# Both layers of a spiking feed-forward network as three products of rounded parts

## The chip, the cores and the metric

One core of a Trainium2 chip. The kernel is one launch; its time is the device time in microseconds. The kernel before has a median of 658.88 us over 3 runs (658.28 to 659.46).

## The reference, cut to what matters

The model is two layers of a perceiver on x (16 x 64 x 256) with a context (16 x 1601 x 256): cross attention, a Mamba block, a spiking feed-forward network; then windowed attention over heads, a second attention, and eight experts of which two are added per token. The change is in the spiking network:

```python
h = jnp.square(jax.nn.relu(jnp.einsum('bsd,fd->bsf', x, W_fc)))   # x is layernormed; f = 1024
y = jnp.einsum('bsf,df->bsd', h, W_proj)                           # d = 256
def step(mem, _):
    reset = spike_fn(mem - 1.0)
    mem_new = 0.9 * mem + y - reset * 1.0
    return mem_new, spike_fn(mem_new - 1.0)
# five steps from mem = 0; the mean of the spikes is added to x
```

A spike is a comparison with a threshold, so y is wanted at nearly float32 precision.

## The kernel before, in words

The 1024 tokens are 8 tiles of 128; a quarter is two tiles (256 tokens, QT). One function, ffn_and_heads, holds the spiking network, the norms on either side and the attention over heads, because the engines work on all of it side by side. Each engine has one program, written out by hand in order at the end of its block; the engines meet only through counters: pe_steps, ac_steps and ve_steps list the order in which TensorE, ScalarE and VectorE complete their steps, and a wait names a step of such a list. GpSimd counts in s_z (its memsets), s_sn and s_v2.

Per quarter q the network goes so:

- TensorE turns the normed tokens of the quarter (turn_normed2, L1475) into a bank; ScalarE moves them to k.xT (move_turned2, L1822).
- TensorE's first_layer(q) (L1496) makes four blocks p = 4q to 4q+3 of 2 x 128 hidden features by 256 tokens, two float32 matmuls of 256 columns for each 128 features, in the two halves of one bank in turn. Block p waits for the relu of block p - 2.
- ScalarE's squares(q) (L1827) takes a relu (L1833) of the bank and writes its square (L1837) into hT, of which there are two. Squares of p wait for those of p - 2.
- TensorE's second_layer(q) (L1512) waits for the last square of the quarter and runs 2 x 8 float32 matmuls of 256 columns. ScalarE moves y (move_y, L1839).
- VectorE runs the five spike steps on y (spike, L2066, in five parts: 14 instructions of 128x512, most with two inputs in SBUF), adds them to x, takes the statistics (deviations3, L2100) and normalises (normalise3, L2109), which feeds the attention over heads.

Before it, VectorE adds the output of the Mamba block (residual2, L2035; deviations2, L2046) and normalises with two tensor_scalars a quarter (normalise2, L2055, instruction L2062). Quarters 0 and 1 come first; the projections of quarters 2 and 3 (out_proj, L1466) are done in this block, quarter 2 ahead of everything and quarter 3 behind first_layer(0).

The attention's own work is woven in: TensorE projects keys (L1522), values (L1535) and queries (project, L1556); VectorE adds the biases (keys, queries, L2122 to L2131); GpSimd multiplies with the sines and cosines (turn_pairs, L1991, three instructions a tile at L1999 to L2001, waiting for the queries' bias and running up to LEAD = 3 tiles ahead); VectorE adds the two products (rotate, L2133); TensorE turns them (turn_rotated, L1568). From step(0) (L1780) a pipeline over tiles i does scores, softmax and weighted values; the last quarter's spikes are run between its first steps. TensorE's order around the change stands at L1749 to L1787:

```python
            out_proj(2); turn_normed2(0); turn_normed2(1); first_layer(0); turn_normed2(2); out_proj(3)
            turn_value_bias(); second_layer(0); project_keys(0); project_value_bias(); first_layer(1)
            turn_normed2(3); project_values(0); second_layer(1); first_layer(2); turn_normed3(0)
            project_keys(1); project(0); second_layer(2); project(1); first_layer(3); turn_rotated(0, 0)
            turn_normed3(1); second_layer(3); turn_rotated(0, 1); project(2); turn_rotated(1, 0)
```

(one call a line in the code). The weights w_fc and w_pr (1 MB each) are loaded by SP long before, during the Mamba block. The experts at the end of the kernel (product, L2588; w_lo on GpSimd at L2847, on VectorE at L2864; rest_of_hidden, L3023) already use three products of rounded parts: a = hi + lo, with hi the value rounded to float32r by ScalarE and lo the rest, and a * b taken as hi*hi + hi*lo + lo*hi.

Of the kernel before, what the change touches and what calls it, by code (L numbers as in the profile page):

```python
# [6 lines left out]
F32 = mybir.dt.float32  # L7
# [7 lines left out]
P = 128  # L15
# [17 lines left out]
FF = 1024  # L33
# [1290 lines left out]
LEAD = 3  # L1324


def ffn_and_heads(nc, k):
# [7 lines left out]
    with ExitStack() as ctx:  # L1335
        sb, ps, sem = tools(nc, ctx)
        r_sb = [sb(f"r{i}", [P, 2, QT]) for i in range(2)]
        hT = [sb(f"fhT{i}", [P, FM, QT]) for i in range(2)]
# [18 lines left out]
        qT = [sb(f"q4T{i}", [P, HC, P]) for i in range(4)]  # L1357
        kT = [sb(f"k4T{i}", [P, HC, P]) for i in range(4)]
        mx = [sb(f"hmx{i}", [P, H]) for i in range(2)]
        sm = [sb(f"hsm{i}", [P, H, L]) for i in range(2)]  # L1360
        pT = sb("hpT", [P, H // 2, P])
# [49 lines left out]
        normed = (T[0], X, O, T[1])  # L1411
        n_pairs = float(L * L)
# [9 lines left out]
        sq = lambda q: [(w, 4 * q + n) for n in range(4) for w in ("re", "sq")]  # L1422
# [5 lines left out]
        ac_steps = [("r2", 1), ("x2", 0), ("x2", 1), ("r2", 2), *sq(0), ("x2", 2), ("cv", 0), ("r2", 3), ("y", 0),  # L1428
# [3 lines left out]
        ve_steps = [("rs", 1), ("st2", 1), ("ag2", 1), ("ep2", 1), ("rc2", 0), ("xn2", 0), ("rc2", 1), ("xn2", 1), ("rs", 2), ("st2", 2), ("ag2", 2),  # L1432
                    ("ep2", 2), ("rc2", 2), ("xn2", 2), ("rs", 3), ("st2", 3), ("ag2", 3), ("ep2", 3), ("rc2", 3), ("xn2", 3),
                    ("k", 0), ("cvec", 0), ("st3", 0), *nm(0), ("st3", 1), *nm(1), ("st3", 2), *nm(2), ("k", 1), ("k", 2),
# [22 lines left out]
        def _(e):  # L1457
# [25 lines left out]
            def turn_value_bias():  # L1483
                ac("x2", 1)
# [1881 lines left out]
```

## Time and profile before

| | before |
|---|---|
| median of 3 runs | 658.88 us |
| the profiled execution | 657.73 us |
| its span | 656.0 us |
| TensorE busy | 602.4 us (92%) |
| VectorE busy | 465.2 us (71%) |
| ScalarE busy | 368.7 us (56%) |
| GpSimd busy | 235.1 us (36%) |

The profile is one execution, and its span is what the engines' records cover; 1.73 us lie around it, and the execution is 1.15 us under the median of the runs. A float32 matmul of the program appears as two records of TensorE, a rounded one (float32r) as one; the type in a matmul's row reads f32 for both. PE is TensorE, PEld its weight loads, DVE VectorE, ACT ScalarE, POOL GpSimd. The name before the arrow is what is written: fhT is hT, hS the banks of both layers, r the relu, xz and mem the spikes' states. The block of ffn_and_heads begins at 369.9 us, its network ends at 444.8, the attention over heads at about 523.

### The profile page before, as it was taken

How to read it: one execution, taken by the hardware profiler on the slowest of the kernel's cores; microseconds unless marked ns; L12 is line 12 of the kernel's file. 1: busy time of each engine (PE TensorE's matmuls, PEld its weight loads, DVE VectorE, ACT ScalarE, POOL GpSimd, SP SyncE). 2: the span in 40 equal slices, each digit the busy share in tenths (PEclk: the TensorE clock that was granted, in tenths of full speed). 3: DMA queues.
4: the chain of work that ended last, by engine and by line, in shares of the span. 5: the costliest groups of instructions: out<-in, count | busy, mean ns of one | idle time of the engine just before them, and what ended most of it. 6: DMA issues, size and time to landing. Idle time of an engine off the chain costs nothing. (4 is left out here: it accounts for less than half of the span.)

```text
span 656.0 us, 11718 instructions
## 1 busy us (share of the span) xinstructions
PE 602.4 (92%) x4436; PEld 460.0 (70%) x4436; DVE 465.2 (71%) x798; ACT 368.7 (56%) x700; POOL 235.1 (36%) x190
## 2 busy tenths in 40 slices
PE   7999999999998778878788999999999899999997
PEld 6645555464366667767677888887777768889897
DVE  2753433347767999999999517788978878886554
ACT  2311111136889999999999333344656465555343
POOL 2000000000089999999898200035651022231000
PEclk8999999999999999999999999999999999999999
DMA  9999999984903232233220000000100022210001
GB/s 335 407 415 416 416 418 414 420 324 159 258 12 107 106 104 97 97 98 126 99 97 1 1 1 17 1 0 19 36 2 2 1 65 85 61 49 1 32 1 33
DMA packets 32831, 87.52 MB, mean 133 GB/s; under 512 B 8092, under 2 KB 20840, under 8 KB 30600
## 3 DMA queue, kind: packets, MB, share of 16 engines
q1 hardware_dynamic: 32088, 86.18, 35.7%
q8 instruction: 36, 0.59, 0.4%
q10 hardware_dynamic: 688, 0.59, 0.3%
q14 instruction: 19, 0.16, 0.1%
HBM read 84.53 MB, written 1.11 MB: 131 GB/s over the span
## 5 line engine op out<-in xcount | busy, mean ns | idle before, releaser
L847 POOL TENSOR_TENSOR dbu<-du,bs 128x1024 f32<-128x1024 f32 x64 | 149.8, 2365 | 7.0 <-DVE w_in L1095 4.6
L976 ACT ACTIVATE weighed<-T,CT 128x256 f32<-128x256 f32 x222 | 94.9, 592 | 1.2 <-PE T L1174 0.9
L1095 DVE TENSOR_TENSOR_SCAN w_in<-hS,dbu 128x1024 f32<-128x1024 f32 x42 | 94.6, 2271 | 0.4 <-ACT hS L965 0.4
L965 ACT ACTIVATE hS<-delta,negA 128x504 f32<-128x504 f32 x128 | 90.7, 813 | 5.3 <-DVE xn L1095 2.5
L1188 PE MATMUL Y<-ident,weighed 128*128 128x128 f32 x512 | 66.8, 273 | 0.1
L1174 PE MATMUL T<-ident,w_in 128*128 128x128 f32 x336 | 45.9, 279 | 19.8 <-ACT weighed L976 13.8
L1188 PEld LDWEIGHTS Y<-ident,weighed 128*128 128x128 f32 x512 | 57.8, 141 | 0.9 <-DVE sres L1119 0.3
L1174 PEld LDWEIGHTS T<-ident,w_in 128*128 128x128 f32 x336 | 36.1, 140 | 30.7 <-DVE w_in L1095 27.4
L1095 DVE TENSOR_TENSOR_SCAN xn<-hS,dbu 128x1024 f32<-128x1024 f32 x22 | 50.0, 2274 | 2.3 <-ACT hS L965 2.3
L425 POOL COPY w_xp<-w_xp 128x64 f32<-128x64 f32 x3 | 0.6, 234 | 138.8 <-DMA w_out<-in_w_out 138.8
L314 PE MATMUL O<-cN,pT 123*64 123x256 f32 (+1 forms) x384 | 46.7, 385 | 3.8 <-DMA cN<-in_ctx 3.1
L452 ACT ACTIVATE prob<-S,nbias 128x1601 f32<-128x1601 f32 x8 | 12.8, 1597 | 58.9 <-DVE nbias L601 58.9
L300 PE MATMUL S<-cT,qkT 128*64 128x512 f32 (+1 forms) x256 | 44.8, 502 | 0.9 <-DMA cT<-in_ctxT 0.7
L2784 ACT ACTIVATE hid<-BK,cols 128x512 f32<-128x512 f32 x32 | 22.0, 689 | 38.1 <-PE BK L2616 37.0
L3028 DVE TENSOR_TENSOR h_lo<-hid,h_hi 128x512 fp32r<-128x512 f32 x32 | 22.1, 693 | 28.6 <-ACT h_hi L2784 28.6
L314 PEld LDWEIGHTS O<-cN,pT 123*64 123x64 f32 (+1 forms) x384 | 25.4, 136 | 18.9 <-DMA cN<-in_ctx 5.0
L300 PEld LDWEIGHTS S<-cT,qkT 128*64 128x64 f32 x256 | 16.3, 136 | 30.1 <-issue 28.1
L2590 PE MATMUL BK<-w_hi,h_hi 128*128 128x256 f32 x128 | 37.1, 290 | 0.1
L594 DVE TENSOR_REDUCE mx<-S 128x1 f32<-128x1601 f32 x8 | 14.6, 1824 | 31.6 <-PE S L300 31.6
L2847 POOL TENSOR_TENSOR w_lo<-raw_w,w_hi 128x512 fp32r<-128x512 f32 x14 | 18.0, 1299 | 52.9 <-ACT w_hi L2727 52.9
L2590 PE MATMUL BK<-w_lo,h_hi 128*128 128x256 f32 x128 | 36.2, 283 | 0.0
L2590 PE MATMUL BK<-w_hi,h_lo 128*128 128x256 f32 x128 | 36.2, 283 | 0.0
(444 smaller groups left out, 1340.7 us busy)
## 6 DMA issues: line engine op xcount, KB each, us to landing
cN<-in_ctx SPq DMA_DIRECT2D x8, 3072.0 KB, 24.3
cT<-in_ctxT SPq DMA_DIRECT2D x7, 3202.0 KB, 24.5
bs<-b_rows SPq DMA_DIRECT2D x32, 512.0 KB, 3.7
raw_w<-in_w SPq DMA_DIRECT2D x16, 256.0 KB, 3.0
cT<-in_ctxT SPq DMA_DIRECT2D x1, 2178.0 KB, 12.2
cR<-in_ctx SPq DMA_DIRECT2D x8, 256.0 KB, 23.7
w<-in_w SPq DMA_DIRECT2D x7, 256.0 KB, 7.9
vs<-vx SPq DMA_DIRECT2D x8, 136.0 KB, 2.4
```

Of the source, the lines that this page charges most:

```text
L300: j = e.matmul(S[64 * b:64 * b + 64, c * HALF:c * HALF + w], qkT[:, kt, q:q + 64], cT[r][:, b, kt, c * HALF:c * HALF + w], start=kt == 0, ...
L314: j = e.matmul(O[64 * b:64 * b + 64, 0:D], pT[0:n_keys(c), c, 64 * b:64 * b + 64], v, start=c == 0, stop=c == ROWS)
L847: e.tensor_tensor(dbu[s % NB][:, :, :], half(m.du, s // DS), row, ALU.mult).then_inc(s_bu, 1)
L965: i = e.activation(by_batch(A[s % 2][:, j * HALF:(j + 1) * HALF]), by_batch(m.delta[:, c, h * HALF:(h + 1) * HALF]), ACT.Exp, scale=m.negA ...
L976: i = e.activation(weighed[s % 2][:, q * Q:(q + 1) * Q], T[:, q * Q:(q + 1) * Q], ACT.Copy, scale=c_of(s, q))
L1095: e.tensor_tensor_scan(S[s % NS], A[s % 2][:, :], dbu[s % NB][:, :, :].rearrange("p c n -> p (c n)"), 0.0, ALU.mult, ALU.add).then_inc(s_h, 1)
L1174: i = e.transpose(T[:, q * Q + j * P:q * Q + (j + 1) * P], S[s % NS][:, j * HALF + q * P:j * HALF + (q + 1) * P], k.ident[:, :])
L1188: i = e.matmul(Y[:, j * HALF + q * P:j * HALF + (q + 1) * P], weighed[s % 2][:, q * Q + j * P:q * Q + (j + 1) * P], k.ident[:, :], start=u ...
L2590: ins = e.matmul(dst, a, b, start=first and i == 0, stop=last and i == 2)
L2784: i = e.activation(dst, HB[m][:, :], ACT.Relu, bias=col(k, "b1", 2 * x + m))
L2847: e.tensor_tensor(k.w_lo[j // 2][:, j % 2, :, :], k.raw[j % SLOTS_W][:, :, :], k.w_hi[j // 2][:, j % 2, :, :].bitcast(F32), ALU.subtract). ...
L3028: e.tensor_tensor(h_lo[n % 2][:, m, :], hid[m][:, :], h_hi[n % 2][:, m, :].bitcast(F32), ALU.subtract).then_inc(s_l, 1)
```

## The change

Both layers are made of three products of rounded parts. Weights: ScalarE copies w_fc and w_pr rounded (fc_hi, pr_hi), GpSimd subtracts (fc_lo, pr_lo, four parts each). Tokens: ScalarE moves the turned tokens rounded (xT_hi), VectorE subtracts from the bank (low_part). Hidden features: ScalarE takes the relu, writes its square rounded (h_hi) and then unrounded over the relu; VectorE (10 blocks) or GpSimd (6 blocks: 4, 5, 8, 9, 12, 13) subtracts (low_square). There is one h_hi and one h_lo for all quarters, so squares of a quarter wait for the second layer of the quarter before. The second layer starts on the first rounded squares instead of the last, and asks for the rest block by block. The new tiles lie where later tiles of the attention lie, or over existing ones; the order of steps in the three lists changes with it.

```diff
+LO_AT = {p: 14 + i for i, p in enumerate((4, 5, 8, 9, 12, 13))}
...
+            fc_hi = part("fc_hi", [P, KD, FF], F32R)
+            x2_lo = [part(f"x2_lo{i}", [P, KD, QT], F32R) for i in range(2)]
+            pr_hi = part("pr_hi", [P, FM, D], F32R)
...
-        hT = [sb(f"fhT{i}", [P, FM, QT]) for i in range(2)]
+        h_hi, h_lo = (sb(n, [P, FM, QT], F32R) for n in ("fh_hi", "fh_lo"))
...
+        def lo_done(e, p):
+            if ("lo", p) in ve_at:
+                e.wait_ge(s_fv, ve_at["lo", p])
+            else:
+                e.wait_ge(s_z, LO_AT[p])
...
             def first_layer(q):
                 tok = slice(q * QT, (q + 1) * QT)
                 ac("x2", q)
+                ac("whi", 0)
...
-                        m = 2 * n + u
+                        cols = slice((2 * n + u) * P, (2 * n + u + 1) * P)
+                        dst = fp[p % 2][:, u * QT:(u + 1) * QT]
                         for c in range(KD):
-                            j = e.matmul(fp[p % 2][:, u * QT:(u + 1) * QT], k.w_fc[:, c, m * P:(m + 1) * P],
-                                         k.xT[:, c, tok], start=c == 0, stop=c == 1)
+                            e.matmul(dst, fc_hi[:, c, cols], k.xT_hi[:, c, tok], start=c == 0, stop=False)
+                            if q == 0 and u == 0 and c == 0:
+                                e.wait_ge(s_z, 4 + p)
+                            e.matmul(dst, k.fc_lo[:, c, cols], k.xT_hi[:, c, tok], start=False, stop=False)
+                        if n == 0 and u == 0:
+                            ve("xl", q)
+                        for c in range(KD):
+                            j = e.matmul(dst, fc_hi[:, c, cols], x2_lo[q % 2][:, c, :], start=False, stop=c == 1)
                     done(j, "fc", p)
...
             def second_layer(q):
-                ac("sq", 4 * q + 3)
                 if q >= 2:
                     ac("y", q - 2)
                 for u in range(2):
+                    dst, tok = yp[q % 2][:, u * D:(u + 1) * D], slice(u * P, (u + 1) * P)
                     for m in range(FM):
-                        j = e.matmul(yp[q % 2][:, u * D:(u + 1) * D], hT[q % 2][:, m, u * P:(u + 1) * P], k.w_pr[:, m, :],
-                                     start=m == 0, stop=m == FM - 1)
+                        if u == 0 and m % 2 == 0:
+                            ac("hi", 4 * q + m // 2)
+                            if q == 0:
+                                e.wait_ge(s_z, 8 + m // 2)
+                        e.matmul(dst, h_hi[:, m, tok], pr_hi[:, m, :], start=m == 0, stop=False)
+                        e.matmul(dst, h_hi[:, m, tok], k.pr_lo[:, m, :], start=False, stop=False)
+                    for m in range(FM):
+                        if u == 0 and m % 2 == 0:
+                            lo_done(e, 4 * q + m // 2)
+                        j = e.matmul(dst, h_lo[:, m, tok], pr_hi[:, m, :], start=False, stop=m == FM - 1)
...
             def squares(q):
...
                     if p >= 2:
-                        e.wait_ge(s_fa, ac_at["sq", p - 2])
-                    done(e.activation(r_sb[p % 2][:, :, :], fp[p % 2].rearrange("p (u n) -> p u n", u=2), ACT.Relu), "re", p)
-                    if q >= 2:
-                        pe("pr", q - 2)
+                        lo_done(e, p - 2)
+                    r = r_sb[p % 2][:, :, :]
+                    done(e.activation(r, fp[p % 2].rearrange("p (u n) -> p u n", u=2), ACT.Relu), "re", p)
+                    if q:
+                        pe("pr", q - 1)
                     e.wait_ge(s_fa, ac_at["re", p])
-                    done(e.activation(hT[q % 2][:, 2 * n:2 * n + 2, :], r_sb[p % 2][:, :, :], ACT.Square), "sq", p)
+                    done(e.activation(h_hi[:, 2 * n:2 * n + 2, :], r, ACT.Square), "hi", p)
+                    e.wait_ge(s_fa, ac_at["hi", p])
+                    done(e.activation(r, r, ACT.Square), "sq", p)
...
+            e.wait_ge(k.s_w3, k.n_w3)
+            done(e.activation(fc_hi[:, :, :], k.w_fc[:, :, :], ACT.Copy), "whi", 0)
             root2(1)
+            done(e.activation(pr_hi[:, :, :], k.w_pr[:, :, :], ACT.Copy), "whi", 1)
             move_turned2(0)
...
+            e.wait_ge(s_fa, ac_at["whi", 0])
+            for n in range(FM // 2):
+                cols = slice(2 * n * P, (2 * n + 2) * P)
+                e.tensor_tensor(k.fc_lo[:, :, cols], k.w_fc[:, :, cols], fc_hi[:, :, cols].bitcast(F32),
+                                ALU.subtract).then_inc(s_z, 1)
+            e.wait_ge(s_fa, ac_at["whi", 1])
+            for n in range(FM // 2):
+                ms = slice(2 * n, 2 * n + 2)
+                e.tensor_tensor(k.pr_lo[:, ms, :], k.w_pr[:, ms, :], pr_hi[:, ms, :].bitcast(F32), ALU.subtract).then_inc(s_z, 1)
             e.wait_ge(s_fp, pe_at["out", 3])
             for r in range(2):
                 e.memset(v2[r][:, :, :, :, :], 0.0).then_inc(s_z, 1)
...
-            for t in range(LEAD):
+            for q in (1, 2):
+                for n in range(2):
+                    low_square(4 * q + n)
+            turn_pairs(0)
+            for n in range(2):
+                low_square(12 + n)
+            for t in range(1, LEAD):
                 turn_pairs(t)
...
+            def low_part(q):
+                ac("x2", q)
+                if q >= 2:
+                    pe("fc", 4 * (q - 2) + 3)
...
+            def low_square(p):
+                q, n = divmod(p, FM // 2)
+                ms = slice(2 * n, 2 * n + 2)
+                ac("sq", p)
+                if q:
+                    pe("pr", q - 1)
+                done(e.tensor_tensor(h_lo[:, ms, :], r_sb[p % 2][:, :, :], h_hi[:, ms, :].bitcast(F32), ALU.subtract), "lo", p)
```

VectorE's order gets low_part(0) and (1) behind the residual of quarter 2, low_square(0) to (3) behind the normalising of quarter 2, low_part(2) behind that of quarter 3, low_part(3) behind normalise3(0), and low_square(6), (7), (10), (11), (14), (15) between the last parts of the spikes of quarters 0, 1 and 2: 6, 10 and 14 ahead of 7, 11 and 15, with one part of the spikes between the two of a pair. The waits of TensorE on a token move ("x2") that guard a bank become waits on the subtraction ("xl") that now reads it last.

## Rows read from the trace of the kernel before

**Rows 1.** Page, part 1: the engines' busy time, share and instructions.

```profile
PE 602.4 (92%) x4436; PEld 460.0 (70%) x4436; DVE 465.2 (71%) x798; ACT 368.7 (56%) x700; POOL 235.1 (36%) x190
```

**Rows 2.** Stretches, all engines: length, busy us (instructions) of PE, PEld, DVE, ACT, POOL, clock, DMA.

```profile
375.00:446.00 71.00, 70.46 (x338) 61.63 (x338) 44.34 (x94) 27.19 (x50) 7.62 (x8) 1.00 0.02 5
...
474.00:520.00 46.00, 44.32 (x673) 35.33 (x674) 35.53 (x81) 27.02 (x44) 12.04 (x27) 1.00 0.01 2
```

**Rows 3.** Timeline of TensorE, first layer of quarter 1: start, us, engine, line, operation.

```profile
395.55 7.07 PE L1508 MATMUL hS<-xT,w_fc 128*128 128x256 f32 x32
402.45 0.60 PE L1479 MATMUL hT<-ident,xn 128*128 128x128 f32 x4
```

**Rows 4.** Timeline of TensorE, an expert's second layer: its first row, the row behind it.

```profile
590.07 0.28 PE L2590 MATMUL BK<-w_hi,h_hi 128*128 128x256 f32 x1
...
592.95 1.03 PE L2570 MATMUL BK<-ident,xn 128*128 128x128 f32 x8
```

**Rows 5.** Timeline of ScalarE, a block's relu and square, and the next relu.

```profile
397.47 0.60 ACT L1833 ACTIVATE r<-hS 128x512 f32<-128x512 f32 x1 [3.72 <-PE hS L1508]
398.11 0.63 ACT L1837 ACTIVATE fhT<-r 128x512 f32<-128x512 f32 x1
```

**Rows 6.** ScalarE, one line's durations (ns, least/median/most), then a row of its timeline.

```profile
L2727 ACT ACTIVATE w_hi<-raw_w x16: 612/626/654, 533.1 to 595.5; 128x512 fp32r<-128x512 f32 x16
...
455.92 1.06 ACT L1885 ACTIVATE hsm<-hsm 128x1024 f32<-128x1024 f32 x1
```

**Rows 7.** Two lines' durations in the experts, ns least/median/most: subtractions of VectorE, of GpSimd.

```profile
L3028 DVE TENSOR_TENSOR h_lo<-hid,h_hi x32: 681/693/716, 544.4 to 647.8; 128x512 fp32r<-128x512 f32 x32
...
L2847 POOL TENSOR_TENSOR w_lo<-raw_w,w_hi x14: 1263/1284/1456, 534.8 to 596.2; 128x512 fp32r<-128x512 f32 x14
```

**Rows 8.** Timeline of GpSimd, then of VectorE beside it, at 555 us.

```profile
554.79 4.02 POOL L2847 TENSOR_TENSOR w_lo<-raw_w,w_hi 128x512 fp32r<-128x512 f32 x3 [7.89 <-ACT w_hi L2727]
...
556.28 1.40 DVE L2909 SCALAR_TENSOR_TENSOR ady<-cn,ady 128x256 f32<-128x256 f32 x1
...
559.13 0.42 DVE L2914 TENSOR_TENSOR ok<-ok,causal 128x256 f32<-128x256 f32 x1
```

**Rows 9.** Timeline of GpSimd, then of VectorE beside it, at 434 us.

```profile
433.29 1.68 POOL L1999 TENSOR_TENSOR w_in<-qkb,trig 128x512 f32<-128x512 f32 x1 [5.75 <-DVE qkb L2130]
...
433.73 1.79 DVE L2089 SCALAR_TENSOR_TENSOR xz<-mem,xz 128x512 f32<-128x512 f32 x1
...
436.68 1.10 DVE L2083 SCALAR_TENSOR_TENSOR xz<-mem,y 128x512 f32<-128x512 f32 x1
```

**Rows 10.** Timelines at the start: VectorE, TensorE, ScalarE.

```profile
372.03 0.73 DVE L2062 TENSOR_SCALAR xn<-x,mv,rstd 128x256 f32<-128x256 f32 x2
...
374.08 0.60 PE L1479 MATMUL hX<-ident,xn 128*128 128x128 f32 x4
374.93 7.17 PE L1508 MATMUL hS<-xT,w_fc 128*128 128x256 f32 x32 [0.25 <-ACT xT L1824]
...
374.28 0.60 ACT L1824 ACTIVATE xT<-hT 128x512 f32<-128x512 f32 x1 [2.12 <-PE hT L1479]
```

**Rows 11.** Timeline of VectorE from y of quarter 1 to that of quarter 2's spikes.

```profile
412.36 0.69 DVE L2083 SCALAR_TENSOR_TENSOR xz<-y 128x512 f32<-128x512 f32 x1 [5.57 <-ACT y L1843]
...
427.58 0.76 DVE L2139 TENSOR_TENSOR hrot<-w_in 128x256 f32<-128x256 f32 x2 [2.81 <-POOL w_in L2001]
429.20 0.69 DVE L2083 SCALAR_TENSOR_TENSOR xz<-y 128x512 f32<-128x512 f32 x1 [0.86 <-ACT y L1843]
...
438.31 0.68 DVE L2090 SCALAR_TENSOR_TENSOR mem<-mem,xz 128x512 f32<-128x512 f32 x1
```

**Rows 12.** Kernel's start: stretches (columns as in rows 2).

```profile
8.00:10.00 2.00, 1.81 (x14) 1.82 (x15) 1.63 (x8) 0.77 (x2) 0.00 (x0) 0.85 1.07 420
10.00:12.00 2.00, 2.00 (x7) 1.64 (x6) 1.17 (x4) 0.48 (x2) 0.00 (x0) 0.50 1.01 405
12.00:14.00 2.00, 1.97 (x10) 1.44 (x9) 0.07 (x1) 0.65 (x2) 0.00 (x0) 0.79 1.01 394
```

More of the change, by code:

```diff
@@ L1336, in ffn_and_heads @@
         sb, ps, sem = tools(nc, ctx)
+        with ExitStack() as before_heads:
+            part = tools(nc, before_heads)[0]
+            fc_hi = part("fc_hi", [P, KD, FF], F32R)
+            x2_lo = [part(f"x2_lo{i}", [P, KD, QT], F32R) for i in range(2)]
+            pr_hi = part("pr_hi", [P, FM, D], F32R)
+        late = sb("qk4T", [P, 4, HC, P])
+        sm = [sb(f"hsm{i}", [P, H, L]) for i in range(2)]
+        pT = sb("hpT", [P, H // 2, P])
         r_sb = [sb(f"r{i}", [P, 2, QT]) for i in range(2)]
-        hT = [sb(f"fhT{i}", [P, FM, QT]) for i in range(2)]
+        h_hi, h_lo = (sb(n, [P, FM, QT], F32R) for n in ("fh_hi", "fh_lo"))
         y = [sb(f"y{i}", [P, 2 * D]) for i in range(2)]
@@ L1356, in ffn_and_heads @@
         rot = [sb(f"hrot{i}", [P, 2 * H, SPAN]) for i in range(2)]
-        qT = [sb(f"q4T{i}", [P, HC, P]) for i in range(4)]
-        kT = [sb(f"k4T{i}", [P, HC, P]) for i in range(4)]
+        qT = [sb(f"q4T{i}", [P, HC, P]) for i in range(2)] + [late[:, i, :, :] for i in range(2)]
+        kT = [sb(f"k4T{i}", [P, HC, P]) for i in range(2)] + [late[:, 2 + i, :, :] for i in range(2)]
         mx = [sb(f"hmx{i}", [P, H]) for i in range(2)]
-        sm = [sb(f"hsm{i}", [P, H, L]) for i in range(2)]
-        pT = sb("hpT", [P, H // 2, P])
         warm = sb("hwarm", [P, 1])
@@ L1421, in ffn_and_heads @@
         fc = lambda q: [("fc", 4 * q + n) for n in range(4)]
-        sq = lambda q: [(w, 4 * q + n) for n in range(4) for w in ("re", "sq")]
+        sq = lambda q: [(w, 4 * q + n) for n in range(4) for w in ("re", "hi", "sq")]
         nm = lambda q: [("ag3", q), ("ep3", q), ("rc3", q), ("xn3", q), ("cx", q)]
@@ L1526, in project_keys @@
                 else:
-                    ac("x2", 2)
+                    ve("xl", 2)
                 for u in range(2):
@@ L1535, in project_values @@
             def project_values(p):
-                ac(*(("x2", 0), ("x3", 1), ("x3", 2), ("v", 2))[p])
+                if p == 0:
+                    ve("xl", 0)
+                else:
+                    ac(*(("x3", 1), ("x3", 2), ("v", 2))[p - 1])
                 for u in range(2):
@@ L1823, in move_turned2 @@
                 pe("t2", q)
-                done(e.activation(k.xT[:, :, 2 * q * P:(2 * q + 2) * P].rearrange("p c (u n) -> p c u n", u=2),
+                done(e.activation(k.xT_hi[:, :, 2 * q * P:(2 * q + 2) * P].rearrange("p c (u n) -> p c u n", u=2),
                                   normed[q][:, :].rearrange("p (u c n) -> p c u n", u=2, c=KD), ACT.Copy), "x2", q)
@@ L2040, in residual2 @@
                 done(e.tensor_tensor(x, x, fp[1] if g == 1 else normed[g][:, :], ALU.add), "rs", g)
+                if g == 2:
+                    low_part(0)
+                    low_part(1)
                 own("rs", g)
@@ L2280, in _ @@
                 normalise2(q)
+                if q == 2:
+                    for n in range(FM // 2):
+                        low_square(n)
+            low_part(2)
             spike(0, 0)
@@ L2287, in _ @@
             spike(0, 3)
+            low_square(6)
             spike(0, 4)
+            low_square(7)
             deviations3(0)
             normalise3(0)
+            low_part(3)
             spike(1, 0)
@@ L2293, in _ @@
             spike(1, 2)
+            low_square(10)
             spike(1, 3)
+            low_square(11)
             spike(1, 4)
@@ L2303, in _ @@
             spike(2, 2)
+            low_square(14)
             spike(2, 3)
+            low_square(15)
             spike(2, 4)
@@ L3111, in perceiver @@
         k.xn = sb("xn", [P, TILES, D])
+        with ExitStack() as rounded:
+            k.xT_hi = tools(nc, rounded)[0]("xT_hi", [P, KD, TOK], F32R)
         k.xT = sb("xT", [P, KD, TOK])
@@ L3258, in perceiver @@
         k.c0T = sb3("c0T", [P, KD, TOK])
+        with ExitStack() as rounded:
+            k.fc_lo = tools(nc, rounded)[0]("fc_lo", [P, KD, FF], F32R)
         k.w_fc = sb3("w_fc", [P, KD, FF])
+        with ExitStack() as rounded:
+            k.pr_lo = tools(nc, rounded)[0]("pr_lo", [P, FM, D], F32R)
         k.w_pr = sb3("w_pr", [P, FM, D])
```

26 lines of the change are left out of this document (19 added, 7 removed).

## The prediction

> **What bounds the kernel now.** I read the page's shares first: TensorE is busy 92% of the span [rows 1]. Then the stretches: in 375 to 446 us, which holds both layers of the spiking network, TensorE works 70.46 of 71.00 us, VectorE 44.34, ScalarE 27.19, GpSimd 7.62 at full clock; in the attention steps behind it (474 to 520 us) TensorE still works 44.32 of 46.00 [rows 2]. So a microsecond taken from or added to TensorE's path there reaches the end: the blocks behind start when this one ends, and I found nothing with slack between. Last the timelines, for what stands beside TensorE: VectorE waits for y of each quarter, then runs its own chain (spikes, normalising, rotation), and waits again. That slack is what the change spends.
>
> **TensorE's own term.** A group of one layer and quarter is 16 float32 matmuls of 256 columns, seen as 32 records; groups follow each other after 6.90 us [rows 3], 0.431 each. The change makes them 48 rounded ones of the same shape. The experts' second layer has exactly these: 24 between 590.07 and 592.95, 0.120 each [rows 4]. So 5.76 us a group, 1.14 less; eight groups give -9.1 us if nothing else binds. The Trainium skill (TensorE: Matmul & The Clock Gate, Back-to-back issue gap) gives N/2.4 + 2.5 ns, 109 ns at 256 columns; the row says 120, and by 109 the sum below would end near 1 us lower. The row decides.
>
> **ScalarE.** Relu takes 0.60, its square 0.63, each waiting for the one before [rows 5]: 1.23 a block. With the second square a block takes 0.64 + 0.66 + 0.54 (the next relu starts while the last square ends) = 1.84, against TensorE's new 1.44. New too are two copies of 128x2048. From 0.626 for 512 columns rounded [rows 6] and 1.06 for 1024 [rows 6], 0.9 ns a column: 2.0 us each. ScalarE is idle then, so the first runs 369.9 to 371.9, the second to 374.1, just ahead of the first move of turned tokens at 374.28 [rows 10]: cost nothing, and without that cover 2 us each.
>
> **GpSimd and VectorE get in each other's way, and this decides.** GpSimd gets 8 subtractions of weights and 6 of squares, 1.28 us each; VectorE 10 of squares at 0.69 (0.60 apart) [rows 7], and 4 of the transposed tokens at the same. While GpSimd ran three of its subtractions back to back (554.79 to 558.81, 1.34 each), a 256-column instruction of VectorE took 1.40 instead of the 0.42 of the one behind them [rows 8]: one GpSimd instruction is let by for one of VectorE's, in turn. The same in this stage: with GpSimd's three products at 433.29, three 0.68 us instructions of VectorE, the first 1.79 and the third 1.10 long, took from 433.73 to 437.78 [rows 9], 4.05 us instead of 1.9 at 0.60 apart: a loss of 2.1. So each 1.28 us subtraction on GpSimd costs VectorE 1.0 to 1.2 where VectorE reads two tensors of SBUF or runs a tensor_scalar, nothing where it reads PSUM. The Trainium skill (SBUF — State Buffer) tells it as an exclusive lock held for a whole instruction, which speaks against this change; the rows agree, so it changes no number.
>
> **The walk.** I follow TensorE's order and carry the shift against before.
> 1. Start. GpSimd's first subtraction begins at 371.94 behind the first copy, VectorE's normalising at 372.03 [rows 10]. Its four tensor_scalars each wait for one GpSimd instruction: 1.0 + 1.2 + 1.0 + 1.2 = 4.3, less 0.4 that they stood ready before the transposes. The second transposes come at 377.9 instead of 374.08 and stand ahead of the first layer, which starts at 378.35 instead of 374.93: **+3.4**. Bounds: 0 if VectorE always goes first, 4.3.
> 2. Quarter 0. Residual 2 and its statistics are behind these and two token subtractions, so the root and with it the first relu come 1 us after the matmuls, and ScalarE's 1.84 a block then leads: the first layer gains nothing (+3.4). Second layer: -1.1, **+2.2**.
> 3. Quarter 1. First layer -1.1. Two GpSimd subtractions (blocks 4, 5) hold the spikes up by 2, and blocks 6 and 7 stand in VectorE's order; block 7 is ready at 409.8, TensorE wants it at 408.2: 1.6 of waiting against 1.1 of gain. **+1.6**.
> 4. Quarter 2. First layer -1.1 (+0.4); then the query projection waits for the tokens' move, queued on ScalarE behind 4 x 1.84: +1.8. Second layer -1.1: **+1.1**. First layer of quarter 3: -1.1, +0.5 for the queries of tile 0: **+0.4**.
> 5. Second layer of quarter 3. It needs VectorE's blocks 14 and 15, after the spikes of quarter 2. VectorE from y of quarter 1 to that place took 412.36 to 438.91 = 26.6 us, with 0.86 of waiting for y that goes [rows 11] (the 2.81 behind GpSimd's products stays). It adds four subtractions of its own (2.4), 2.0 for GpSimd's blocks 8 and 9, 2.1 for 12 and 13, 0.3 around. From 413.8 that gives 446.3, where TensorE waits since 440.1. 26 matmuls remain, 3.1: done issuing at 449.4 instead of 444.7: **+4.8**.
> 6. The rotation of tile 2 and the keys come late behind the spikes of quarter 3: +0.9, after that the steps keep the shift: **+5.8**.
> 7. Clock. TensorE has two thin stretches, 373.5 to 378.35 and 440.1 to 446.3. At the kernel's start, behind waits for the first loads, the granted clock fell to 0.85, 0.50 and 0.79 of full in three stretches of 2 us [rows 12], 2 x (0.15 + 0.50 + 0.21) = 1.7 us lost between its levels of 2.4 and 1.2 GHz. Bounds 0 and 2 x 1.7 here; I take one fall, at the second and longer stretch, part of it spent in the wait: **+1.2**.
>
> Costs of nothing: the weight parts are there before they are used (first at 373.2 wanted at 378.5, last of the second layer at 382.8 wanted at 390.7); TensorE's new waits on copies and token parts fall behind later ones; the memsets of v2 keep their place after the projection; GpSimd's rotation of tile 0 stands behind blocks 8 and 9, done at 419.8, before its queries, and tile 1 behind 12 and 13 is part of step 5. No DMA is added or moved; SP waits on the moved values as before.
>
> **Sum.** +5.8 + 1.2 = +7.0: span 656.0 to 663.0, the profiled execution 657.73 to 664.7; it stood 1.15 under the median of 658.88, so 665.9.
>
> **Rivals.**
> A, VectorE first: if the first copy ends after 372.03, or VectorE's instruction wins the tie, one or two of the four waits at the start go. For it: 0.09 us decides. +3.7 to +4.9 before the clock: 662.6 to 663.8.
> B, VectorE keeps up in quarter 3: GpSimd and VectorE overlap more than rows 9 show, so step 1 or step 5 loses its waiting. Walked with one of the two free, the shift is +1.5 to +2.5: 660.4 to 661.4. Against it: both rows show whole turns.
> C, faster: the turns hardly cost, the rounded matmuls pay. The turns are some 11 us of new waiting on VectorE (4.3 at the start, 1.1 behind it, 2.0, 2.1, the rest smaller); the sign changes once more than about 6 of them are gone, and with none at all the walk ends 6.2 to 8.4 under: 650.5 to 652.7. For it: all 32 of VectorE's subtractions in the experts took 0.68 to 0.72 [rows 7]. Against: GpSimd did nothing beside them, and where it did [rows 8, 9] the turns are whole.
> D, the clock falls twice, or long after the second stretch: +8.5 to +10: 667.4 to 669. The Trainium skill (TensorE: Matmul & The Clock Gate, HAM oscillation) has idle gaps in TensorE's work fall back to half clock, each time again; here that is D in full.
> E, the rounded products are not at 0.120: at 0.125 it is +0.5, at 0.108 -1.2; inside the forecast.
>
> **Chances.** Forecast 0.56, A 0.12, B 0.12, D 0.10, C 0.10. The range runs from B's lower middle to D: 660.8 to 669.0; it leaves out C, half of B's edge and D's tail. A measurement here can tell 0.2%, 1.3 us, from no change. Faster by more: C, 0.10. Within: B's lowest, 0.04. Slower: the rest, 0.86.
>
> **What would show it.** Step 1: normalising at L2062's place with durations of 1.3 to 1.6 us, and the first layer at 378. Step 3: TensorE waiting about 1.6 us for a subtraction of VectorE. Step 5: a wait of about 4 us and one of about 1.7 in the last second layer, released by VectorE, spikes at 1.1 to 1.8 us. Step 7: granted clock under 1.00 behind it. TensorE's groups at 5.76 where nothing waits. I am wrong if the waits at L2062's place stay at 0.41, if the last second layer runs through, or if a group takes more than 6.9 us unbroken.

## The result, and the profile after

| | before | after |
|---|---|---|
| median | 659.14 us (658.28 to 659.46, 4 runs) | 664.94 us (664.60 to 665.55, 4 runs) |
| the profiled execution | 657.73 us | 664.60 us |
| its span | 656.0 us | 662.6 us |

The ratio of after to before is 1.0094, 95% interval 1.0082 to 1.0107: 0.9% slower, 1 us under the forecast of 665.9 and inside its range. The profiled executions differ by 6.87: 6.6 of span and 0.27 around it. Before's profiled execution was quicker than its median, so medians differ by 5.8 only.

The page of the changed kernel, its shares and the granted clock in 40 slices (compare [rows 1]):

```profile
PE 599.8 (91%) x4564; PEld 462.9 (70%) x4564; DVE 484.2 (73%) x812; ACT 381.4 (58%) x718; POOL 254.6 (38%) x204
...
PEclk9999999999999999999999899988999999999999
```

The stretch of both layers (columns as in [rows 2]):

```profile
375.00:446.00 71.00, 60.29 (x439) 57.49 (x440) 57.70 (x100) 35.40 (x64) 23.26 (x20) 0.94 0.02 5
```

TensorE has lost what bound it: 60.29 busy of 71 us where it had 70.46, while VectorE went from 44.34 to 57.70. Where it went, in the timeline of the start; ScalarE, GpSimd, VectorE, TensorE, and ScalarE's first blocks:

```profile
369.44 1.91 ACT L1963 ACTIVATE fc_hi<-w_fc 128x2048 fp32r<-128x2048 f32 x1 [0.47 <-PEq L706]
...
371.43 5.09 POOL L2026 TENSOR_TENSOR fc_lo<-w_fc,fc_hi 128x512 fp32r<-128x512 f32 x4 [0.28 <-ACT fc_hi L1963]
...
371.53 2.60 DVE L2146 TENSOR_SCALAR xn<-x,mv,rstd 128x256 f32<-128x256 f32 x2
...
374.23 2.44 DVE L2146 TENSOR_SCALAR xn<-x,mv,rstd 128x256 f32<-128x256 f32 x2
...
374.18 0.66 PE L1495 MATMUL hT<-ident,xn 128*128 128x128 f32 x4 [0.88 <-DVE xn L2146]
376.72 1.11 PE L1495 MATMUL hX<-ident,xn 128*128 128x128 f32 x4 [1.89 <-DVE xn L2146]
377.49 0.56 PE L1526 MATMUL hS<-xT_hi,fc_hi 128*128 128x256 f32 x1
...
380.49 0.58 ACT L1869 ACTIVATE r<-hS 128x512 f32<-128x512 f32 x1
381.10 0.63 ACT L1873 ACTIVATE fh_hi<-r 128x512 fp32r<-128x512 f32 x1
381.76 0.63 ACT L1875 ACTIVATE r<-r 128x512 f32<-128x512 f32 x1
382.30 0.58 ACT L1869 ACTIVATE r<-hS 128x512 f32<-128x512 f32 x1
```

VectorE normalises with two pairs of instructions. A pair took 0.73 us before [rows 10]; now the two take 2.60 and 2.44 us beside GpSimd's row of subtractions. TensorE waits 0.88 and 1.89 us for them and starts the first layer at 377.49; it was 374.93 [rows 10], in a block that began 0.5 us later (VectorE's first instruction there is at 369.96 before, at 369.46 after).

Then quarters 1 to 3: two groups of the first layer with what stands behind each, TensorE's waits for low parts, and VectorE beside GpSimd:

```profile
396.68 0.47 PE L1526 MATMUL hS<-xT_hi,fc_hi 128*128 128x256 f32 x1
...
402.55 0.60 PE L1495 MATMUL hT<-ident,xn 128*128 128x128 f32 x4
...
409.01 0.51 PE L1551 MATMUL hS<-pr_hi,fh_lo 128*128 128x256 f32 x2 [1.51 <-DVE fh_lo L2114]
...
412.18 0.28 PE L1526 MATMUL hS<-xT_hi,fc_hi 128*128 128x256 f32 x1
...
417.86 0.60 PE L1587 MATMUL hT<-ident,xn 128*128 128x128 f32 x4
...
443.47 0.80 PE L1551 MATMUL hS<-pr_hi,fh_lo 128*128 128x256 f32 x2 [3.84 <-DVE fh_lo L2114]
445.40 0.79 PE L1551 MATMUL hS<-pr_hi,fh_lo 128*128 128x256 f32 x2 [1.13 <-DVE fh_lo L2114]
445.99 0.41 PE L1546 MATMUL hS<-pr_hi,fh_hi 128*128 128x256 f32 x1
...
433.48 1.46 POOL L2071 TENSOR_TENSOR fh_lo<-r,fh_hi 128x512 fp32r<-128x512 f32 x1 [2.02 <-ACT r L1875]
435.35 1.29 POOL L2071 TENSOR_TENSOR fh_lo<-r,fh_hi 128x512 fp32r<-128x512 f32 x1 [0.41 <-ACT r L1875]
438.33 1.68 POOL L2049 TENSOR_TENSOR w_in<-qkb,trig 128x512 f32<-128x512 f32 x1 [1.69 <-DVE qkb L2214]
...
433.82 1.67 DVE L2167 SCALAR_TENSOR_TENSOR xz<-mem,y 128x512 f32<-128x512 f32 x1
435.42 1.77 DVE L2173 SCALAR_TENSOR_TENSOR xz<-mem,xz 128x512 f32<-128x512 f32 x1
...
438.76 1.79 DVE L2173 SCALAR_TENSOR_TENSOR xz<-mem,xz 128x512 f32<-128x512 f32 x1
440.48 1.20 DVE L2174 SCALAR_TENSOR_TENSOR mem<-mem,xz 128x512 f32<-128x512 f32 x1
441.72 1.09 DVE L2167 SCALAR_TENSOR_TENSOR xz<-mem,y 128x512 f32<-128x512 f32 x1
442.73 0.68 DVE L2114 TENSOR_TENSOR fh_lo<-r,fh_hi 128x512 fp32r<-128x512 f32 x1
...
444.65 0.69 DVE L2114 TENSOR_TENSOR fh_lo<-r,fh_hi 128x512 fp32r<-128x512 f32 x1
```

The groups run in 5.87 and 5.68 us where 6.90 stood [rows 3]. Each GpSimd subtraction makes one spike instruction of VectorE 1.7 to 1.8 us instead of 0.69, and the three rotation products three more. Blocks 14 and 15 are subtracted at 442.73 and 444.65; TensorE, which has run out of other matmuls by 439.6, waits 3.84 and 1.13 us. Behind that its matmuls are 0.21 apart: half clock.

### The profile page after: what moved, and what is told of

Same layout as the page of the kernel before. It is cut to its first block and busy times, and to the rows that moved or that the text cites. A ratio compares the mean times of both kernels' runs of the same rounds, so it can differ in the third digit from the quotient of the medians.

```text
span 662.6 us, 12043 instructions
## 1 busy us (share of the span) xinstructions
PE 599.8 (91%) x4564; PEld 462.9 (70%) x4564; DVE 484.2 (73%) x812; ACT 381.4 (58%) x718; POOL 254.6 (38%) x204
## 3 DMA queue, kind: packets, MB, share of 16 engines
HBM read 84.53 MB, written 1.11 MB: 129 GB/s over the span
```

## The experiments

How far each kernel's events lie behind those of the kernel before, in us, from ScalarE's timeline of each profile: y of quarters 0 to 3, the first exponential of the heads (455.92 before), the second move of v (531.03), the turned phases' move (562.41), and the span (656.0). The column "start" has the first instruction of VectorE in the block of the network (369.96 before): nothing that was edited comes before it, it differs between profiles by itself, and every later column contains it. The names are those of the experiments below.

| profile | start | y0 | y1 | y2 | y3 | first exp | v | phases | span |
|---|---|---|---|---|---|---|---|---|---|
| after | -0.50 | +1.32 | +0.65 | +0.51 | +6.42 | +6.54 | +6.59 | +6.59 | +6.6 |
| start_later | -0.49 | -1.97 | -2.62 | -2.77 | +2.07 | +2.08 | +3.12 | +4.60 | +4.6 |
| weights_memset | -0.50 | -1.44 | -2.10 | -2.23 | +2.52 | +2.52 | +3.51 | +4.99 | +4.9 |
| all_memset | -0.32 | -1.74 | -3.64 | -4.06 | -2.59 | -2.57 | -1.59 | -0.10 | -0.1 |
| clock_fill | -0.26 | +1.53 | +0.89 | +2.30 | +3.97 | +4.79 | +4.81 | +6.29 | +6.2 |
| first_only | +0.13 | +3.43 | +2.21 | +0.99 | -0.24 | -0.24 | +0.81 | +0.81 | +0.8 |
| first_later | -0.14 | -0.82 | -2.04 | -3.26 | -4.49 | -4.48 | -3.43 | -3.40 | -3.4 |
| second_only | +0.09 | -1.13 | -1.80 | -1.92 | +3.52 | +3.53 | +4.57 | +4.60 | +4.6 |
| ve_all | +0.03 | -1.43 | -3.88 | -1.53 | -1.49 | -0.53 | +0.52 | +2.04 | +2.0 |
| before_again | -0.15 | -0.16 | -0.16 | -0.16 | -0.16 | -0.15 | -0.12 | +1.35 | +1.3 |
| after_again | -0.35 | +2.53 | +1.88 | +3.32 | +6.82 | +6.83 | +7.90 | +7.89 | +7.9 |
| first_later_fill | -0.14 | -0.81 | -2.04 | -3.27 | -4.51 | -4.50 | -4.50 | -4.50 | -4.5 |
| before_shift | +0.72 | +2.27 | +2.27 | +2.28 | +2.27 | +2.27 | +2.27 | +3.79 | +3.8 |

Read it in two halves. Up to the first exponential the columns tell what the edit does, mixed with the falls of the clock in that stretch. From there on all kernels run the same work (first_later_fill has its transposes at the end of the block besides), and the shift still grows by 1.0 at v or by 1.5 at the phases in some profiles and not in others; that is the clock, below.

### start_later: the weights' remainders wait for the normalising

```diff
             e.wait_ge(s_fa, ac_at["whi", 0])
+            e.wait_ge(s_fv, ve_at["xn2", 1])
             for n in range(FM // 2):
                 cols = slice(2 * n * P, (2 * n + 2) * P)
```

> The eight weight subtractions of GpSimd wait until VectorE has normalised quarters 0 and 1; nothing else is changed. Theory of the turns: in the changed kernel VectorE's four normalising instructions take 2.60, 2.60, 2.44 and 2.44 us beside these subtractions (0.7 before), and the first layer of quarter 0 begins at 377.49 instead of 374.93 less 0.5. Without them beside, VectorE's four are back at 0.41 each, the walk of the orders gives 3.8 us less than the changed kernel, and the stretch of a low granted clock at 376 to 380 has no wait ahead of it any more: 660.3 to 661.3. Rival, ScalarE is the bound (three activations for each block, 1.82 us): it starts no later and then sets the pace, so what is won at the start is lost by the end of quarter 1: 664 to 665. Rival, the granted clock alone: the gain is that of the first low stretch, below 1 us.

Measured: 662.97 us (before beside it 658.31), ratio 1.0072 [1.0054, 1.0091]. The timeline of VectorE and GpSimd at its start:

```profile
371.54 0.73 DVE L2147 TENSOR_SCALAR xn<-x,mv,rstd 128x256 f32<-128x256 f32 x2
...
372.38 0.73 DVE L2147 TENSOR_SCALAR xn<-x,mv,rstd 128x256 f32<-128x256 f32 x2
...
373.27 5.01 POOL L2027 TENSOR_TENSOR fc_lo<-w_fc,fc_hi 128x512 fp32r<-128x512 f32 x4 [2.10 <-DVE xn L2147]
```

Both pairs are back at 0.73. At the first exponential the kernel is 4.46 us ahead of the changed one, +2.08 against before, or +2.57 counted from the block's start; the walk gave +2.0. ScalarE as the bound of the whole is out: the lead at the start (3.29 us at y of quarter 0) is still 3.27 and 3.28 at those of quarters 1 and 2. The turns of the weights are not gone but moved: the pair that normalises quarter 2 now takes 2.21 us, the first low square 1.78. The time fell less than expected, by some 1.5 us (1.0094 to 1.0072; the two intervals overlap, so the medians alone hardly tell it), to 1.7 us above the top of what was expected, and the table says where: +1.04 and +1.48 came back in the experts, where nothing was edited.

### weights_memset and all_memset: the same places, no operand read

```diff
-                e.tensor_tensor(k.fc_lo[:, :, cols], k.w_fc[:, :, cols], fc_hi[:, :, cols].bitcast(F32),
-                                ALU.subtract).then_inc(s_z, 1)
+                e.memset(k.fc_lo[:, :, cols].bitcast(F32), 0.0).then_inc(s_z, 1)
```

and the same for pr_lo; in all_memset also for h_lo in GpSimd's low_square. These kernels leave the low parts out of the result.

> Leaves out the remainders of the weights: GpSimd writes zeros where it subtracted, eight times, with the same semaphores; TensorE's work is the same. Theory of the turns: an instruction that only writes does not hold VectorE up, so the four normalising instructions take about 0.41 us each and the time is that of the kernel whose subtractions start later, 660.3 to 661.3. If a write of zeros holds VectorE up like a subtraction, the time stays at 664 to 665.

> Leaves out the remainders of the weights and of six of the sixteen squares: GpSimd writes zeros in place of all fourteen subtractions, same semaphores, same work on TensorE and ScalarE. Theory of the turns: no spike instruction of VectorE is over 0.75 us between 395 and 445, blocks 14 and 15 come in time, and the walk gives 9 us less than the changed kernel: 655 to 657, below the kernel before. Rival, ScalarE's third activation is the bound: its block of 1.82 us is unchanged, so 660 to 662, the gain of the start alone.

Measured: weights_memset 662.70, ratio 1.0063 [1.0046, 1.0079]; all_memset 657.98, ratio 0.9986 [0.9971, 1.0001], 1.4 and 1.0 us above what was expected. Weights_memset, GpSimd and VectorE at the start:

```profile
371.41 2.21 POOL L2026 MEMSET fc_lo<- 128x512 f32 x4 [0.25 <-ACT fc_hi L1963]
...
371.53 1.62 DVE L2145 TENSOR_SCALAR xn<-x,mv,rstd 128x256 f32<-128x256 f32 x2
...
373.26 1.11 DVE L2145 TENSOR_SCALAR xn<-x,mv,rstd 128x256 f32<-128x256 f32 x2
```

and all_memset, GpSimd and VectorE in quarter 2:

```profile
430.71 0.53 POOL L2070 MEMSET fh_lo<- 128x512 f32 x1 [1.34 <-ACT r L1875]
431.20 1.47 POOL L2048 TENSOR_TENSOR w_in<-qkb,trig 128x512 f32<-128x512 f32 x1
...
430.82 0.68 DVE L2172 SCALAR_TENSOR_TENSOR xz<-mem,xz 128x512 f32<-128x512 f32 x1
431.42 1.80 DVE L2173 SCALAR_TENSOR_TENSOR mem<-mem,xz 128x512 f32<-128x512 f32 x1
...
434.28 1.21 DVE L2113 TENSOR_TENSOR fh_lo<-r,fh_hi 128x512 fp32r<-128x512 f32 x1
```

TensorE's waits for VectorE's low parts in all_memset, from 368 to 460 (total, times, longest):

```profile
PE hS L1551 <- DVE fh_lo L2113: 2.2, 3, 1.4
```

The expectation was half wrong: a memset of 0.54 us does hold up a tensor_scalar (the four lost 1.3 us in all; beside subtractions 3.6), but not a two-input spike instruction (0.68 beside the memset, 1.80 beside the product). From weights_memset to all_memset only the six squares change, and the first exponential comes 5.1 us sooner: those turns were the larger part. With both gone the kernel is 2.57 ahead of before at that place (2.25 from the block's start; walk 3.2), not the 9.1 of TensorE's own term. Part of the rest is in the profile: the rotation products still make spike instructions of 1.80 and 1.10 us and a low square of 1.21, against the 0.75 that was expected at most, TensorE still waits 2.2 us for VectorE's low parts, and the clock fell behind these waits (0.53 at 438 to 441). How much ScalarE's block of 1.82 us and VectorE's ten subtractions keep by themselves is not shown.

### first_only, first_later, second_only: one layer at a time

In first_only the second layer is the old one; first_later adds the wait of start_later; second_only has the old first layer.

```diff
-            h_hi, h_lo = (sb(n, [P, FM, QT], F32R) for n in ("fh_hi", "fh_lo"))
+            hT = [sb(f"fhT{i}", [P, FM, QT]) for i in range(2)]
...
-                        e.matmul(dst, h_hi[:, m, tok], pr_hi[:, m, :], start=m == 0, stop=False)
-                        e.matmul(dst, h_hi[:, m, tok], k.pr_lo[:, m, :], start=False, stop=False)
+                        j = e.matmul(yp[q % 2][:, u * D:(u + 1) * D], hT[q % 2][:, m, u * P:(u + 1) * P], k.w_pr[:, m, :],
+                                     start=m == 0, stop=m == FM - 1)
```

> The change for the first layer alone: rounded parts of its weight and its input as in the changed kernel; the second layer is the kernel before's float32 one (one square, two hT buffers, no low squares, no rounded w_pr), and the start is not delayed. Theory of the turns: the start loses 3.0 us to the four subtractions of w_fc beside VectorE's normalising, the first layers of quarters 1 to 3 win 1.14 us each, and VectorE has only four instructions more, so the second layer of quarter 3 waits for nobody: the walk gives 0.5 us less than the kernel before at the end of the stretch, 657 to 659.5 with one fall of the clock at the start. Rival, the square's three activations and the second layer's products were what paid: then first-layer products alone give no gain over the changed kernel, 663 to 666.

> As the kernel with the change for the first layer alone, and GpSimd's four weight subtractions wait until VectorE has normalised quarters 0 and 1. Theory of the turns: the start costs nothing and each of the four first layers wins about 1.1 us; the walk gives 4.3 us less than the kernel before at the end of the stretch: 653.5 to 655.5, and up to 2.5 more where the granted clock falls at 525 and 557 us, as it did in three kernels whose stretch ended at another time than those of the kernels before and changed: at most 658. Rival, first-layer products don't pay: 658 or more with no fall.

> The change for the second layer alone: rounded w_pr, three activations for a block, sixteen low squares on VectorE and GpSimd in the places that the changed kernel gives them; the first layer is the kernel before's float32 one with no rounded input or weight. Theory of the turns: the start is free, but VectorE and GpSimd hold each other up in quarters 1 to 3 as in the changed kernel and TensorE waits for the low parts of blocks 14 and 15: the walk gives 2.5 us more than the kernel before, and the fall of the clock at that wait 1 to 2.5 more: 661 to 663.5. Rival, the loss is the start's alone: at or below the kernel before, 655 to 659.

Measured beside a before of 659.13: first_only 658.66, ratio 0.9998 [0.9982, 1.0014]; first_later 654.87, ratio 0.9944 [0.9925, 0.9963]; second_only 663.14, ratio 1.0071 [1.0047, 1.0096]. At the first exponential -0.24, -4.48 and +3.53 stand beside the walk's -0.5, -4.3 and +2.5, the last without the fall of the clock that its expectation put at 1 to 2.5 more. The stretch of first_later, and TensorE's waits in second_only from 368 to 460 (total, times, longest):

```profile
375.00:438.00 63.00, 62.41 (x384) 57.33 (x384) 44.13 (x89) 25.60 (x47) 11.26 (x11) 1.00 0.02 5
```

```profile
PE hS L1542 <- DVE fh_lo L2089: 4.9, 3, 3.5
```

With the first layer alone TensorE hardly waits (62.41 busy of 63.00 us) and for no low part: all four groups' 1.14 arrive, 4.5 us, and VectorE has four instructions more instead of fourteen. With the second layer alone the wait of quarter 3 is there without any trouble at the start. So the change is two: a half that pays, once its start is delayed, and a half that costs, in this order of the engines' work.

### ve_all: all sixteen low squares on VectorE

The wait of start_later, no low_square on GpSimd, and VectorE's order so (q1, for example):

```diff
             spike(1, 0)
+            low_square(8)
             spike(1, 1)
             spike(1, 2)
-            low_square(10)
+            low_square(9)
             spike(1, 3)
-            low_square(11)
             spike(1, 4)
+            low_square(10)
             deviations3(1)
+            low_square(11)
             normalise3(1)
```

> Both layers as in the changed kernel; GpSimd's weight subtractions wait for the normalising of quarters 0 and 1, and all sixteen low squares are VectorE's, spread over its order a little after the blocks (GpSimd has none). VectorE has six instructions of 0.69 us more than in the changed kernel (4.1 us). Theory of the turns: each of GpSimd's 1.28 us subtractions cost VectorE 1.0 to 1.2 us, so giving them up costs VectorE nothing, and the order brings blocks 14 and 15 sooner: the walk gives 1.9 us less than the kernel before at the end of the stretch, 656 to 658, up to 2.5 more with falls of the clock later. Rival, VectorE's load is the bound, whoever holds it up: 4.1 us more than the kernel whose subtractions start later (663.0), 665 to 667.

Measured: 657.47 (655.57 to 660.14 in ten runs), ratio 0.9979 [0.9960, 0.9998]. Giving VectorE 4.1 us more work of its own made the kernel 5 to 6 us faster than start_later, where it should have slowed it if VectorE's load were the bound. The order was changed with it (the low squares, and the low part of quarter 3's tokens, which moved behind the queries' bias), so how much of this is the turns' alone is not separated here; all_memset is the run for that. TensorE waits for no low part any more; it waits 2.9 us for the move of normed tokens, which stands on ScalarE behind the triple activations. The walk's -1.9 was -0.53: in this profile the clock fell there too, at 417 to 423 and 444 to 450. Beside the same runs of before the first layer alone, started late, has the lower median (0.9944 against 0.9979, intervals that overlap by 0.0003), so no run here shows the second layer's products paying.

### clock_fill: work for TensorE in the wait

```diff
+                        if q == 3 and u == 0 and m in (4, 6):
+                            for _ in range((0, 0, 30, 8)[m // 2]):
+                                e.transpose(fp[0][:, 0:P], k.ident[:, :], k.ident[:, :])
                         if u == 0 and m % 2 == 0:
                             lo_done(e, 4 * q + m // 2)
```

> Adds 38 transposes of the identity into a free PSUM bank, ahead of TensorE's waits for the low parts of blocks 14 (30 of them) and 15 (8) in the second layer of quarter 3; nothing else is changed. Theory that the low clock after that wait (0.90 at 438 to 442, 0.50 at 442 to 449, 0.60 at 449 to 452) costs time of its own: the granted clock stays at 1.00 from 438 to 455, the matmuls behind the wait are back at 0.12 us each, and the time falls by 1.2 to 2.0 us: 663.0 to 663.8. Rival, VectorE is what the end waits for and the slow matmuls lie beside it: within 0.4 us of the changed kernel. The transposes themselves can cost at most 0.5 us, where they run past the end of the wait.

Measured: 665.17, ratio 1.0106 [1.0087, 1.0125]: no gain. Stretches of this kernel (length, busy us of each engine, clock), then those of the changed kernel:

```profile
422.00:428.00 6.00, 5.54 (x30) 5.38 (x31) 5.49 (x15) 0.61 (x2) 0.00 (x0) 0.72 0.01 3
438.00:442.00 4.00, 3.52 (x31) 3.31 (x30) 3.97 (x4) 3.58 (x7) 4.00 (x4) 1.00 0.00 0
442.00:449.00 7.00, 7.00 (x64) 7.00 (x62) 6.59 (x15) 0.30 (x2) 0.36 (x1) 1.00 0.01 2
```

```profile
422.00:428.00 6.00, 5.78 (x45) 5.68 (x46) 5.49 (x14) 0.37 (x2) 0.00 (x0) 1.00 0.01 3
438.00:442.00 4.00, 1.23 (x8) 1.02 (x8) 3.96 (x5) 1.95 (x4) 3.67 (x3) 0.90 0.00 0
442.00:449.00 7.00, 4.40 (x19) 4.11 (x20) 6.56 (x16) 0.20 (x1) 0.26 (x1) 0.50 0.01 2
```

The filled wait keeps the clock, and y of quarter 3 comes 2.45 us sooner, the first exponential 1.75. But in this execution the clock fell at 422 to 428 instead, behind a wait of 2.1 us that the changed kernel has too (2.0) without a fall; that one was hidden in the wait for VectorE. Another 1.5 went at the phases. The pair of profiles prices the fall; the medians don't confirm a gain. The measured time is where the rival of the expectation had it, within 0.4 us of the changed kernel, though its reason, that the slow matmuls lie beside VectorE's work, is not what the profile shows.

### before_again, after_again, before_shift, first_later_fill: when the clock falls

```diff
# before_shift, on the kernel before
             turn_normed2(1)
+            for _ in range(19):
+                e.transpose(T[1][:, 0:P], k.ident[:, :], k.ident[:, :])
             first_layer(0)
# first_later_fill, on first_later, at the end of the block
             turn_normed(3)
+            for _ in range(12):
+                e.transpose(T[0][:, 0:P], k.ident[:, :], k.ident[:, :])
```

> The kernel before, unchanged: a second profiled execution. If whether the granted clock falls at some place depends on the kernel alone, it is 0.57 at 9 to 12 us and 1.00 from 18 us on, as in the first profile, and the span is within 0.3 us of 656.0. If it depends on the execution (the place is the same, the fall comes or not), falls may show at 519 to 533 or 552 to 563 and the span is 1.0 to 2.5 us longer.

> The changed kernel, unchanged, on the chip of this call: 663.5 to 665.5 and a ratio of 1.008 to 1.011. Its second profile has VectorE's four normalising instructions at 2.4 to 2.6 us and TensorE's waits for low parts at 6 to 7 us in all, as they follow from the orders of the engines; whether the clock falls at 375 to 381 and 441 to 452 only, or elsewhere too, is what it is to show.

> The kernel before with 19 transposes of the identity (2.05 us at 0.108) ahead of the first layer of quarter 0: everything behind comes 2.0 us later, and nothing else is changed. If the late falls of the clock (525 to 531, 557 to 563) depend on when a stretch comes and not on what the change does, this kernel shows them as the kernel with the later subtractions did, shifted by 2.1 there: before plus 3.0 to 4.5, 661.5 to 663.5. If not, before plus 2.0: 660.5 to 661.5. If the start has slack, less.

> As the kernel with the change for the first layer alone and the delayed start (654.87), and 12 transposes of the identity into a free PSUM bank at the end of this block's work of TensorE, ahead of the wait of 1.98 us at the border to the next block. Where the clock fell at 519 to 525 behind this wait, it cost 1.0 us between the outputs of v. If work ahead of the wait keeps the clock, 653.5 to 654.3; if the last transpose delays the next block, up to 1.3 us more than without; no difference if the low share of work earlier in the stretch decides.

Measured: before_again 659.08, one execution; after_again 665.69, ratio 1.0091 [1.0074, 1.0107]; before_shift 660.61, ratio 1.0018 [1.0006, 1.0030]; first_later_fill 653.27, ratio 0.9908 [0.9891, 0.9924], beside a before of 659.30. One stretch of the first profile of before, then of its second:

```profile
551.00:557.00 6.00, 6.00 (x35) 4.50 (x34) 4.26 (x7) 2.36 (x5) 2.21 (x2) 1.00 0.01 3
```

```profile
551.00:557.00 6.00, 6.00 (x26) 4.54 (x25) 4.23 (x7) 2.21 (x5) 2.35 (x2) 0.77 0.03 3
```

The same kernel, the same instructions, once at full clock and once with a fall: +1.5 us. TensorE's timeline there, of the second:

```profile
553.35 1.18 PE L2637 MATMUL BK<-b,w_out 8*128 8x256 f32 x4
554.46 0.59 PE L2504 MATMUL BK<-small,same_batch 128*128 128x4 f32 x2
554.91 0.56 PE L2590 MATMUL BK<-w_hi,h_hi 128*128 128x256 f32 x1
555.27 0.41 PE L2590 MATMUL BK<-w_lo,h_hi 128*128 128x256 f32 x1
```

Where it falls is tied to a place, whether it falls is not tied to the kernel. before_shift had that fall too, but its ten runs lie between 659.47 and 662.03 around +1.3, under the 2.05 inserted (the start had some slack: from the block's start y of quarter 0 moved by 1.55): one profile and these times don't bear out the idea that lateness itself brings the falls. after_again repeats the slow normalising (2.61 and 2.43) and TensorE's three waits for low parts, but 4.4 us of them instead of 6.5: the clock fell at 423 to 428 here as well, and TensorE came 2.8 us later (y of quarter 2) to a VectorE whose block 15 was 0.9 later (445.53 for 444.65). So the two slow down beside each other, and y of quarter 3 moved by 0.4 only. The expected 6 to 7 us of waits didn't come, and the median lies 0.2 above the expected times.

In first_later the clock fell behind the wait at the border to the experts' block; the row is TensorE's timeline of first_later_fill, transposes ahead of that wait:

```profile
518.53 1.47 PE L1832 MATMUL hT<-ident 128*128 128x128 f32 x12
520.66 1.15 PE L2560 MATMUL BK<-xT,w_in 128*64 128x64 f32 x32 [0.66 <-PEq L1336]
```

The next block starts at 520.66 as without them (520.70), the clock stays up and the 1.0 us is not lost in this profile. That the transposes did it is not shown by it: the same wait of 1.98 us stands in the other profiles too, and in five of those thirteen the clock stayed up without them. The medians, 0.9944 and 0.9908 of before, were taken on two chips; their intervals don't meet, and its four runs lie within 0.6 us, where the six of first_later spread over 2.8. The two medians differ by more than the 1.0 us of that fall, and the rest is not explained. This version is the best of the study, 0.9% faster than before.

## Why the prediction was right

The numbers of the walk are shifts against before, whose block began 0.5 us later in its profile; 0.5 is added to the measured ones below.

- **TensorE's term.** 0.120 a matmul: 48 in 5.87 and 5.68 us. Right, and rival E with it did not arise. The estimate of 109 ns by the Trainium skill's formula (TensorE: Matmul & The Clock Gate, Back-to-back issue gap) would have made it 5.2; the trace doesn't agree with it.
- **ScalarE.** A block 1.84, measured 1.81 (380.49 to 382.30); the copies 2.0, measured 1.91 and 1.90, covered as said.
- **Step 1.** Four waits, 4.3 us (its four terms add up to 4.4); measured 5.04 for what takes 1.46 alone, 3.6. First layer +3.4, measured +3.1. Rival A is out: the first copy ended at 371.35 and GpSimd began at 371.43, 0.1 us ahead of VectorE's first normalising instruction (371.53). start_later shows what it was worth: 4.46 at the end of the stretch.
- **Steps 2 to 4.** +2.2, +1.6 and +1.1 at the ends of the second layers; by y +1.8, +1.2 and +1.0. The wait of 1.6 for block 7 was 1.51.
- **Step 5.** VectorE's last block 446.3, 445.8 with the block's earlier start; measured end 445.34, waits 3.84 and 1.13 for "about 4 and about 1.7". Right in place, releaser and size. Rival B is out; second_only (+3.53, wait of 3.5) and all_memset (-2.57) name the cause.
- **Step 7 was mis-sized, and step 6 hid it.** I took one fall and 1.2 us. It fell twice: at 375 to 380 (0.66), which the root and ScalarE's longer blocks covered, and behind the wait of quarter 3, where 26 matmuls and y took 6.0 us from 445.34 instead of some 3.4. That is 2.45 at y (clock_fill). Step 6's +0.9 for the rotation and keys came to 0.1, since y itself was late; in clock_fill, where y is in time, it is 0.82. Together +7.04 against my +7.0: two errors that cancel.
- **Rival D** had two falls and 667.4 or more; the two falls came, but only the second had a price. **Rival C**, that the turns hardly cost, is out: they cost 4.5 us (start_later) and 5.1 us (weights_memset to all_memset), with the falls of the clock behind the waits that they made.
- The sum gave 664.7 for the profiled execution, which took 664.60. That it is so close is luck as well: the block began 0.5 us earlier than before's, and 0.27 us more lay outside the span, neither of which the walk had. The 1 us between forecast and median is its last line: I added the profile's 1.15 under the median in full. The median of before probably holds falls of the clock that its profile did not have (before_again, 659.08, has one); the changed kernel's profile was nearer its own median (664.60 and 664.94).

## What to carry to other kernels

Before GpSimd is given work to relieve VectorE, count which VectorE instructions will run beside it: each 1.28 us subtraction there cost VectorE 1.0 to 1.2 us, nearly twice the 0.60 that the same subtraction costs on VectorE itself. A change that touches two places should be walked and tried apart; here one half, started late, gave 0.6%, and the other cost 0.7%. And where TensorE becomes quicker than its feeders, its new waits can have the half clock behind them, as behind the waits at the start and in quarter 3 of both profiles of the changed kernel. With a few transposes into a free bank in such a wait the clock was up behind it in both places tried, one profile each; in one of them it fell elsewhere and no gain was measured, in the other it had often stayed up without them.

## What the hardware showed that I had not expected

- A GpSimd memset, which reads nothing, held up VectorE's tensor_scalar (1.62 and 1.11 us for pairs of 0.73) but not its two-input instruction (0.68). The Trainium skill (SBUF — State Buffer, Who interferes with whom) says just this: two SBUF inputs contend only with a GpSimd instruction that reads, a tensor_scalar in its two-port mode with any. The traces agree; I had not used the distinction.
- The clock falls in executions, not in kernels. At the experts' phases (551 to 563) it fell in seven of the fourteen profiles, always for 1.5 us; behind the border of the blocks in eight, for 1.0. Of the two profiles of before one has the first of these, of the two of the changed kernel one has the second. Ten runs of one kernel spread over 2.6 to 4.6 us (ve_all 655.57 to 660.14, all_memset 655.20 to 659.12); the fastest of ve_all had a mean granted clock of 0.996, the slowest one of 0.986. A single profile can be 1.0 to 2.5 us off by these two falls for no reason that lies in the edit. Compare such kernels stage by stage and take the falls out by the granted clock. The Trainium skill (TensorE: Matmul & The Clock Gate, HAM oscillation) tells of gaps that bring the fall; the traces agree only in part, for the fall at 552 to 558 came without one, TensorE busy 6.00 of 6.00 us; ahead of it stand matmuls of 8 rows and two of 4 columns.
